# Graph attention: wk and wq by blocks of 128 columns, M's four banks filled together, and another order in the last group's splits

## What is computed

```
h     = maximum(layernorm(x), 0)
out   = h @ weight
alpha = (h @ wq) @ (h @ wk).T            # per graph, 128 x 128
alpha = maximum(alpha, 0) * (adj != 0)
alpha = softmax(alpha, axis=1)
return x + alpha @ out
```

## Time and profile before

| what | us |
|---|---|
| median of 3 runs (lowest, highest) | 414.24 (414.03, 414.66) |
| the profiled execution | 414.27 |
| its span | 412.4 |
| PE busy | 405.8 (98% of the span) |
| PE weight loads busy | 321.9 (78%) |
| DVE busy | 298.1 (72%) |
| ACT busy | 277.8 (67%) |
| POOL busy | 264.5 (64%) |

### The profile page before, as it was taken

One profiled execution on the slowest core, in us unless ns is written; L12 is line 12 of the kernel. 1 busy time (PEld: TensorE's weight loads), 2 busy tenths in 40 slices (PEclk: granted clock), 3 DMA queues, 4 the chain that ended last, 5 costly groups with the idle time before them and its releaser, 6 DMA issues.

```text
span 412.4 us, 9484 instructions
## 1 busy us (share of the span) xinstructions
PE 405.8 (98%) x3581; PEld 321.9 (78%) x3581; DVE 298.1 (72%) x569; ACT 277.8 (67%) x590; POOL 264.5 (64%) x284
## 2 busy tenths in 40 slices
PE   8999999999999999999999999999999999999995
PEld 5444545979798897979798797979889797979883
DVE  5797789895867776776767777676777667556565
ACT  4749887766867677766777776776867776643534
POOL 0767896979495876859495775939577584910003
PEclk9999999999999999999999999999999999999999
DMA  8973858998969897896979497896988599393022
GB/s 299 367 98 69 215 105 224 225 206 209 218 170 191 237 155 210 193 206 183 188 219 192 131 240 200 200 214 174 188 252 157 154 219 234 41 187 100 2 103 102
DMA packets 161641, 75.03 MB, mean 182 GB/s; under 512 B 135360, under 2 KB 143808, under 8 KB 161600
## 3 DMA queue, kind: packets, MB, share of 16 engines
q1 hardware_dynamic: 161024, 73.55, 77.4%
q10 hardware_dynamic: 576, 0.92, 0.6%
HBM read 24.12 MB, written 16.78 MB: 99 GB/s over the span
## 4 chain that ended last, share of the span: by engine, by line
PE 82%; DVE 7%; ACT 4%; POOL 3%; issue 2%; DMA 2%; SPq 1%; DVEq 0%; ACTq 0%; POOLq 0%
PE bank L1139 10%; PE bank L1142 10%; PE bank L1141 10%; PE bank L1154 9%; PE bank L1157 9%; PE bank L1156 9%; PE s_bank L1170 3%; PE s_bank L1169 3%; PE s_bank L1168 3%; PE bank L1175 2%; PE bank L1177 2%; PE bank L1176 2%; DMA x_sb<-in_x 2%; POOL hn_lo L417 1%; ACT h L537 1%
## 5 line engine op out<-in xcount | busy, mean ns | idle before, releaser
L417 POOL TENSOR_TENSOR hn_lo<-h,hn_hi 128x512 f16<-128x512 f32 x64 | 74.5, 1174 | 54.0 <-ACT hn_hi L547 53.7
L537 ACT ACTIVATE h<-x_sb,shift,rstd 128x512 f32<-128x512 f32 x64 | 49.9, 804 | 23.6 <-POOL shift L412 23.3
L443 POOL TENSOR_TENSOR hn_lo<-s,hn_hi 128x512 f16<-128x512 f32 x56 | 63.3, 1161 | 0.3 <-ACT hn_hi L552 0.3
L1156 PE MATMUL bank<-wt_lo,hT_hi 128*128 128x256 f16 x224 | 61.1, 273 | 0.0
L1141 PE MATMUL bank<-hT_lo,mt_hi 128*128 128x256 f16 x224 | 61.1, 273 | 0.0
L1154 PE MATMUL bank<-wt_hi,hT_hi 128*128 128x256 f16 x224 | 61.1, 273 | 0.0
L1142 PE MATMUL bank<-hT_hi,mt_lo 128*128 128x256 f16 x224 | 61.1, 273 | 0.0
L1139 PE MATMUL bank<-hT_hi,mt_hi 128*128 128x256 f16 x224 | 61.1, 273 | 0.0
L1157 PE MATMUL bank<-wt_hi,hT_lo 128*128 128x256 f16 x224 | 61.1, 273 | 0.0
L552 ACT ACTIVATE hn_hi<-s 128x512 f16<-128x512 f32 x56 | 33.7, 625 | 24.1 <-POOL s L432 19.7
L1157 PE MATMUL bank<-w_hi,hT_lo 128*128 128x256 f16 x168 | 45.8, 273 | 0.0
(11 more groups left out here) (166 smaller groups left out, 1105.0 us busy)
## 6 DMA issues: line engine op xcount, KB each, us to landing
out_h<-x_sb SPq DMA_DIRECT2D x62, 256.0 KB, 2.1
x_sb<-in_x SPq DMA_DIRECT2D x15, 1024.0 KB, 5.5
adj_sb<-in_adj SPq DMA_DIRECT2D x16, 256.0 KB, 5.3
hn_hi<-in_L_gnn_wq SPq DMA_DIRECT2D x4, 256.0 KB, 5.6
x_sb<-in_x SPq DMA_DIRECT2D x2, 512.0 KB, 7.2
w_sb<-in_L_gnn_weight SPq DMA_DIRECT2D x2, 512.0 KB, 8.6
hn_lo<-in_L_gnn_wk SPq DMA_DIRECT2D x2, 256.0 KB, 3.6
hn_lo<-in_L_gnn_wk ACTq DMA_DIRECT2D x2, 256.0 KB, 3.8
```

The lines of the kernel that those rows point to most:

```text
L417: nc.gpsimd.tensor_tensor(hn_lo[:, s, b], h[:, b], hn_hi[:, s, b], ALU.subtract).then_inc(h_split, 1)
L443: nc.gpsimd.tensor_tensor(low, s32[:, f], high, ALU.subtract).then_inc(s_split, 1)
L537: nc.scalar.activation(h[:, b], x_sb[:, s, b], ACT.Relu, bias=shift[:, b:b + 1], scale=rstd[:, b:b + 1]).then_inc(h_made, 1)
L1156: nc.tensor.matmul(o, ah[:, r, k], bl[:, k], start=False, stop=False, skip_group_check=True)
```

## The change

Seven edits:

1. wk is loaded by SP and wq by ACT, each in four blocks of 128 *columns* (all 512 rows), so in pieces of 512 bytes.
2. PE transposes column block k of wk and of wq together (`transpose_block`) and adds block k's share to all four banks of M (`product_m(k)`, four matmuls). The order is block 0, products 0, blocks 1 and 2, products 1, block 3, products 2 and 3 with the small ops in between. ACT copies wk's and wq's blocks in turn.
3. The transposes use banks VB, VE, FREE and s_bank, the small ops VB, the matmuls on zeros TA.
4. DVE takes the maxima block by block (`w_max` is four times as wide), computes `m_scale` before `w_lo`, and makes `m_lo` directly behind `w_lo`; `out_unscale`, `s_unscale` and the statistics of h(1) come after.
5. T(1) goes to banks TB, TE, FREE, TA (`t_bank`), and waits for three v_lo of group 0, for the fourth only before its last bank; V(1) goes to TB, TE, TA, FREE, with the waits to match.
6. In the last group ACT makes three p_hi, then C12, then C22; DVE does C12 before C22; outputs 0 and 1 wait for two v_lo.
7. In the last group output 1, not 0, goes through ACT and POOL, and ACT issues its store last.

```diff
-            for r in (0, 2):
-                sp.dma_start(wk_sb[:, r], wk[r * N:(r + 1) * N, :]).then_inc(wk_loaded[r], 16)
-            for r in range(K):
-                sp.dma_start(wq_sb[:, r], wq[r * N:(r + 1) * N, :]).then_inc(wq_loaded[r], 16)
+            for k in range(K):
+                sp.dma_start(wk_sb[:, :, k * N:(k + 1) * N], wk_dram[:, :, k * N:(k + 1) * N]).then_inc(wk_loaded[k], 16)
...
         def _(act):
-            for r in (1, 3):
-                act.dma_start(wk_sb[:, r], wk[r * N:(r + 1) * N, :]).then_inc(wk_loaded[r], 16)
+            for k in range(K):
+                act.dma_start(wq_sb[:, :, k * N:(k + 1) * N], wq_dram[:, :, k * N:(k + 1) * N]).then_inc(wq_loaded[k], 16)
...
-            for r in range(K):
-                act.wait_ge(wkT_filled, r + 1)
-                nc.scalar.activation(wkT[:, :, r], wT_bank[r], ACT.Copy).then_inc(wkT_copied, 1)
-            for r in range(K):
-                act.wait_ge(wqT_filled, r + 1)
-                nc.scalar.activation(wqT[:, :, r], wT_bank[r % 2], ACT.Copy).then_inc(wqT_copied, 1)
+            for k in range(K):
+                act.wait_ge(wkT_filled, k + 1)
+                nc.scalar.activation(wkT[:, k], wT_bank[k % 2], ACT.Copy).then_inc(wkT_copied, 1)
+                act.wait_ge(wqT_filled, k + 1)
+                nc.scalar.activation(wqT[:, k], wT_bank[2 + k % 2], ACT.Copy).then_inc(wqT_copied, 1)
...
-            hi_of_p(LAST, range(HG))
+            hi_of_p(LAST, range(HG + 1))
+            hi_of_v12(LAST)
             hi_of_v22(LAST)
-            hi_of_v12(LAST)
-            hi_of_p(LAST, range(HG, GB))
+            hi_of_p(LAST, range(HG + 1, GB))
             hi_of_v21(LAST)
...
+            w_factor, m_factor = 2.0 ** W_SHIFT, W_TOP / (4 * D)
+            nc.vector.scalar_tensor_tensor(m_scale[:], ipow2[:, 1:2], m_factor, ipow2[:, 2:3], ALU.mult,
+                                           ALU.mult).then_inc(scale_step, 1)
+            for k in range(K):
+                vec.wait_ge(w_hi_made, k + 1)
+                nc.vector.scalar_tensor_tensor(w_lo[:, k], w_sb[:, k], w_scale[:], w_hi[:, k], ALU.mult,
+                                               ALU.subtract).then_inc(w_split, 1)
+            vec.wait_ge(scale_step, 5)
+            for k in range(K):
+                vec.wait_ge(m_hi_made, k + 1)
+                nc.vector.scalar_tensor_tensor(m_lo[:, k], M_BANK[k], m_scale[:], m_hi[:, k], ALU.mult,
+                                               ALU.subtract).then_inc(m_split, 1)
             nc.vector.tensor_scalar(out_unscale[:], pow2[:, 0:1], 1.0 / (P_SCALE * H_SCALE * T_SCALE * w_factor), None,
                                     ALU.mult).then_inc(scale_step, 1)
             nc.vector.scalar_tensor_tensor(s_unscale[:], pow2[:, 1:2], 1.0 / (H_SCALE ** 2 * T_SCALE * m_factor),
                                            pow2[:, 2:3], ALU.mult, ALU.mult).then_inc(scale_step, 1)
             for b in range(GB):
                 stats_all(1, 1, b)
...
-            lo_of_v(LAST, 1, c22_v, 1, 1)
-            lo_of_v(LAST, 2, bank[VE][:], 0, 1)
+            lo_of_v(LAST, 1, bank[VE][:], 0, 1)
+            lo_of_v(LAST, 2, c22_v, 1, 1)
...
+            def product_m(k, cs=range(K)):
+                pe.wait_ge(wkT_copied, k + 1)
+                pe.wait_ge(wqT_copied, k + 1)
+                for c in cs:
+                    m = nc.tensor.matmul(M_BANK[c], wqT[:, k, c], wkT[:, k], start=k == 0, stop=k == K - 1)
+                    if k == K - 1:
+                        m.then_inc(m_filled, 1)
...
-            pe.wait_ge(v_split, GB)
             pe.wait_ge(hT_landed[1], 2 * 16)
+            pe.wait_ge(v_split, GB - 1)
             for c in range(K):
+                if c == K - 1:
+                    pe.wait_ge(v_split, GB)
                 whole_product_t(1, c)
...
-                pe.wait_ge(v_split, GB * LAST + (3 if b < HG else 4))
+                pe.wait_ge(v_split, GB * LAST + (2 if b < HG else 4))
```

More of the change, by code:

```diff
@@ L189, in graph_attention_kernel @@
         last_half = [bank[FREE][:, :HD], s_flat[:, :HD]]
-        wT_bank = [bank[k][:].rearrange("p (k n) -> p k n", k=K) for k in (VB, VE, VA, TE)]
-        top_bank = bank[FREE]
+        wT_bank = [b.rearrange("p (r n) -> p r n", r=K) for b in (bank[VB][:], bank[VE][:], bank[FREE][:], s_flat)]
+        top_bank = bank[VB]
         x0_loaded = [sem(f"x0_loaded{k}") for k in range(2)]
@@ L989, in _ @@
             nc.vector.memset(alpha[:, 0:2], 0.0).then_inc(alpha_zeroed, 1)
[L990 to L995, removed]
+            for k in range(K):
+                vec.wait_ge(wk_loaded[k], 16)
+                weight_max(wk_sb[:, :, k * N:(k + 1) * N], w_max[:, 2, k])
+                vec.wait_ge(wq_loaded[k], 16)
+                weight_max(wq_sb[:, :, k * N:(k + 1) * N], w_max[:, 1, k])
             for b in range(GB):
@@ L1017, in _ @@
                                     ALU.mult, ALU.add).then_inc(scale_step, 1)
-            for k in range(K):
-                vec.wait_ge(w_hi_made, k + 1)
-                nc.vector.scalar_tensor_tensor(w_lo[:, k], w_sb[:, k], w_scale[:], w_hi[:, k], ALU.mult,
-                                               ALU.subtract).then_inc(w_split, 1)
             nc.vector.tensor_scalar(ipow2[:].bitcast(I32), pow2[:].bitcast(I32), -1.0, INV_BITS, ALU.mult,
@@ L1033, in _ @@
                 stats_all(1, 1, b)
-            vec.wait_ge(scale_step, 5)
-            for k in range(K):
-                vec.wait_ge(m_hi_made, k + 1)
-                nc.vector.scalar_tensor_tensor(m_lo[:, k], M_BANK[k], m_scale[:], m_hi[:, k], ALU.mult,
-                                               ALU.subtract).then_inc(m_split, 1)
             make_mask(0, 0, 1)
@@ L1102, in _ @@
             lo_of_v(LAST, 0, bank[VA][:], 0, 0)
-            lo_of_v(LAST, 1, c22_v, 1, 1)
-            lo_of_v(LAST, 2, bank[VE][:], 0, 1)
+            lo_of_v(LAST, 1, bank[VE][:], 0, 1)
+            lo_of_v(LAST, 2, c22_v, 1, 1)
             lo_of_v(LAST, 3, bank[VB][:], 1, 0)
-            for b in range(1, GB - 1):
+            for b in (0, 2):
                 residual(LAST, LAST % UNROLL, b)
@@ L1202, in period @@
                 if g == FIRST:
-                    pe.wait_ge(v_split, GB + TA + 1)
+                    pe.wait_ge(v_split, GB + HG + 1)
                 product_t(s, N_P1, bank[TA][:], True)
@@ L1207, in period @@
                 if g == FIRST:
-                    pe.wait_ge(v_split, GB + TE + 1)
+                    pe.wait_ge(v_split, GB + HG)
                 first_use(g, mt_split, T1)
@@ L1289, in whole_product_t @@
                 for k in range(K):
-                    nc.tensor.matmul(M_BANK[c], m_hi[:, k, cols], hT_hi[:, s, 0:GB, k], start=k == 0, stop=False)
-                    nc.tensor.matmul(M_BANK[c], m_hi[:, k, cols], hT_lo[:, s, 0:GB, k], start=False, stop=False)
-                    last = nc.tensor.matmul(M_BANK[c], m_lo[:, k, cols], hT_hi[:, s, 0:GB, k], start=False,
+                    nc.tensor.matmul(t_bank(g)[c], m_hi[:, k, cols], hT_hi[:, s, 0:GB, k], start=k == 0, stop=False)
+                    nc.tensor.matmul(t_bank(g)[c], m_hi[:, k, cols], hT_lo[:, s, 0:GB, k], start=False, stop=False)
+                    last = nc.tensor.matmul(t_bank(g)[c], m_lo[:, k, cols], hT_hi[:, s, 0:GB, k], start=False,
                                             stop=k == K - 1)
@@ L1299, in _ @@
             for k in range(WARM):
-                nc.tensor.matmul(top_bank[:], zeros[:, :N], zeros, start=True, stop=True)
+                nc.tensor.matmul(bank[TA][:], zeros[:, :N], zeros, start=True, stop=True)
             pe.wait_ge(ident_made, 1)
-            for r in range(K):
-                transpose_wk(r)
-            transpose_wq(0)
-            transpose_wq(1)
+            transpose_block(0)
             product_m(0)
-            transpose_wq(2)
-            transpose_wq(3)
+            transpose_block(1)
+            transpose_block(2)
             product_m(1)
+            transpose_block(3)
+            product_m(2, range(1))
             pe.wait_ge(top_step, 1)
             nc.tensor.transpose(top_bank[0:3, 0:N], w_top[:], ident[:]).then_inc(top_filled, 1)
-            product_m(2, range(1))
+            product_m(2, range(1, HK))
             pe.wait_ge(top_step, 3)
@@ L1315, in _ @@
             nc.tensor.matmul(top_bank[:, N:N + 3], ones[:], top_diag[:], start=True, stop=True).then_inc(top_filled, 1)
[L1316 removed]
+            product_m(2, range(HK, K))
             product_m(3)
@@ L1341, in _ @@
             for b in range(GB):
-                pe.wait_ge(t_split, K + b + 1)
+                pe.wait_ge(t_split, K + min(b + 1 + b // HG, GB))
                 whole_product_v(1, b)
```

71 lines of the change are left out of this document (34 added, 37 removed).

## The result

| | before | changed |
|---|---|---|
| median of 5 runs, us | 414.24 (414.03 to 414.66) | 418.54 (417.99 to 418.96) |
| ratio, 95% interval | | 1.0103 (1.0091 to 1.0114) |
| profiled execution, us | 414.27 | 418.15 |
| its span, us | 412.4 | 416.3 |
| PE busy, us | 405.8 | 405.9 |

The change costs 4.3 us of the median, 3.9 us of the profiled span. The forecast was 417.9 (416.3 to 420.5).

A forecast was written before the change was run, and what follows sets the result against it. PE's queue was taken to bound the kernel, so only new PE waits cost time. From 414.24 us, +3.75 (scores) - 0.25 + 0.1 + 0.2 - 0.2 = +3.6 gave 417.9; own range 416.3 to 419.5, 8 in 10 within 416.3 to 420.5.

The forecast's parts named there:

- Loads: DMA of wk and wq in 512-byte pieces at 300 GB/s: block 0 at about 4.5 us, x and w 1.7 later.
- Up to the last copy: PE and ACT: last block copies end at about 17.3 us, so h(0) starts at 17.3, 3.35 us late.
- ACT and DVE to h(1): ACT and DVE queues from h(0): w_hi at 22.2 us, h(1) at 35.7, 4.0 us late.
- To the scores: From h(1) to PE's scores(0): t_split at 48.4 us, scores(0) at 48.5, +3.75 us.
- A wait of some 2 us at t_split: PE at the first scores, on DVE's tT_lo: expected as its longest wait, some 2 us.
- T(1), outputs(0), middle, tail: PE after the scores: T(1) +3.5 us without a wait, outputs(0) +3.6 taken, middle +0.2, tail -0.2.
- PE absorbs everything: h(1) under 0.35 us late, no wait at t_split, PE's own work decides: 414.2 us, no change; 4%.
- Quick tiny ops: DVE's s_unscale costs 0.14 us beside POOL's subtractions, h(1) 1.1 earlier: about +2.5, 416.8 us; 12%.
- A late clock: PE's block 0 products still run at 1.2 GHz, 6.9 us and not 3.45: +7.0, 421.3 us; 10%.
- Small packets at twice the price: DMA's small packets at twice the cost, x and w 3.5 us late: +4.1, 418.4 us; 6%.

The follow-up runs named there:

- a_first: Changed kernel; block 3's transposes before block 1's products, group 0's statistics before wq's last maximum, group 1's directly behind w_lo, unscales last; 414.75 us (1.0017).
- best: Kernel before with the bank and last-group edits and DVE order ipow2, m_scale, w_lo, group 1's statistics, m_lo, unscales; 413.14 us (0.9972).
- b_hold: Kernel before with only four extra ACT copies into an unused buffer ahead of the first h; 415.79 us (1.0044).
- b56: Kernel before with the changed kernel's PSUM bank and last-group edits alone; 413.92 us (0.9996).
- best_gate: Same kernel as best, plus a POOL wait: group 0's second hn_lo waits until DVE has made top_diag; 413.44 us (0.9978).
- experiment 5: The run b_hold: kernel before, with only a delay on ACT ahead of h(0); 415.79 us (1.0044).
- a_dve_old: Changed kernel with DVE's order of before: w_lo, ipow2 and m_scale, unscales, group 1's statistics, then m_lo; 417.66 us (1.0075).

## Why the prediction was right, point by point

- **Loads.** Block 0 at 4.5: PE's first transpose came at 4.25, DVE's first maximum at 4.14. Early by 0.3. For the whole of the loads the price was nearly right: x's statistics were to start 1.7 late and started 1.8 late (12.14 for 10.35). By a_first x itself was 1.4 late (1.1 to 1.9 over the executions), and the other 0.4 is DVE's maximum of wq's last block, for which it waited with x there. The changed kernel's DMA from 2 to 12 us ran at 314 GB/s, before at 372:

```profile
DMA packets 4726, 3.14 MB, mean 314 GB/s; under 512 B 152, under 2 KB 4209, under 8 KB 4726
```

  By the Trainium skill (DMA: Bandwidth & Descriptors, the table at its head) 512 B should have reached line rate; the runs do not agree, and the estimate of 300 was near: from 5 to 8 us, where all packets are small, the rate was 288 to 292. The loads are also shared out otherwise between the two queues, which no run undid by itself.
- **Up to the last copy.** Forecast: products at 7.0, last copies to 17.3, h(0) at 17.3. Measured: 6.61, 17.2, **17.10**.
- **ACT and DVE to h(1).** w_hi 22.2 (21.99), w_lo 22.9 (22.74), s_unscale over 1 us (1.19), h(1) 35.7 (**35.87**). The experiments priced the parts: 0.9 us of time for DVE's order, 1.35 for block 3's transposes, 1.5 for the statistics of group 0 with the third DVE order, and 0.5 left for PE's M phase.
- **To the scores.** +3.75 forecast, +3.91 measured. "A wait of some 2 us at t_split" was 1.8. The forecast put the rest at smaller waits in M and V and left out its largest piece: 1.1 us at the last bank of T(0), which waits for copy_m(3) behind h(1) on ACT. Nothing was lost by the omission, as PE would have stood that time at the scores instead.
- **T(1), outputs(0), middle, tail.** T(1) without a wait, +3.47 (+3.5 forecast); outputs(0) +3.93 (up to 3.75, 3.6 taken); the last group's scores +4.09; then the tail gives back 0.2 (16.48 us from there to the end, for 16.67), as forecast. 0.16 of it is won at the last group's first output, whose wait is 0.19 for 0.35; the forecast had it at 0.1 or less.
- **The rivals.** PE absorbs everything: no, h(1) was 4.2 late. Quick tiny ops: no, s_unscale took 1.19. A late clock: no; block 0's four products took 3.67 us, as fast as those of before at 12.82 (3.60) and so at the 2.4 GHz pace, right behind a hole of 0.79 us, though the four transposes at 4.25 still had the slow one (1.09 us for four, 0.60 at 15.49). Small packets at twice the price: no, x was 1.4 and not 3.5 late.
- **The size of the whole.** The forecast's +3.6 is +3.9 in the profiled span; the term that was small is outputs(0), taken as +3.6 and measured +3.93. The rest of the distance from 417.9 to 418.54 is that this profiled execution lies 0.4 under the median.
- **One step of the reasoning was too narrow.** The prediction measured lateness at the scores. Over the thirteen kernels the span follows h(1) better: in a_first and best the scores are 1.44 and 0.90 late and the span is +0.9 and -0.3, with h(1) at +0.59 and -0.80. Within 0.5 us the span moved with h(1) in every run. PE's lateness at the outputs of group 2 says it more sharply, as it does not change from there to the last group's scores by more than 0.01: in nine kernels it is h(1)'s within 0.11 (4.08 for 4.19 in the changed one, 1.30 for 1.28 in b_hold). In the other four (b56, a_first, best, best_gate) PE has no wait from V(0) on but, at most, the 0.34 us at the last output of group 1 that before has too, so there PE's M phase set the time. The changed kernel has h(1) and the scores late by 4, so it could not tell them apart.

## What to carry to other kernels

When work is cut finer so that one engine can start sooner, follow the in-order queue of the engine that serves it: what stands behind the last small piece there moves too, and may be the head of the longest chain. Before adding a piece to such a queue, delay its next instruction alone, as experiment 5 did, to learn whether it has slack. On an engine that serves several, small operations whose results are needed late belong behind the work that the longest chain waits for, and where they don't run beside another engine's long one.

## What the runs showed of the hardware

- **A tiny DVE operation can wait for a whole POOL operation.** The 3x3 top_diag took 0.22 us free and up to 1.19 beside POOL's hn_lo; the 128x3 pow took 0.17 in a_dve_old, where POOL started behind it, and 0.99 in b_hold, from 17.50 to 18.49, when the first hn_lo, begun at 17.31, was 1.18 old. In these kernels m_scale and s_unscale (1.2 us against 0.15) behave alike. The operations of the same chain that read PSUM did not: w_top<-bank took 0.16 and top_col 0.28 in every trace. Nor did w_scale and out_unscale (0.15), which read a single column. The Trainium skill (SBUF — State Buffer, "SBUF: two separate sides") has an exclusive lock on a port pair of the two engines, held for the full instruction and taken by DVE operations in a 2-port mode or with two SBUF inputs. The traces agree, ends and exceptions alike, though they don't show in which mode a DVE operation ran, and they add that the size of the DVE operation does not matter: an operation of nine elements waits its microsecond.
- **Tenths decide whether it strikes.** In the kernel before top_diag began at 16.88, near the end of the first hn_lo (16.04 + 1.16 = 17.20), and took 0.34. In best it began at 17.25, as the second did (17.26), and took 1.19. PE waited 0.7 us for it there and ACT's w_hi 0.96. A tie can go the other way: in the changed kernel m_scale and the third hn_lo both began at 21.65, and m_scale took 0.16.
